# The Mamba front of a two-layer model on one core: five PSUM banks in a ring, one activation table set, and work for the scan moved ahead of the barrier

## What is computed

```python
xn = _layernorm(x, norm_w, norm_b)
xz = xn @ W_in                                   # 256 -> 2 x 512
x_ssm, z = jnp.split(xz, 2, axis=-1)
xc = conv(x_ssm, conv_w) + conv_b                # 4 taps per channel, causal
x_conv = silu(xc)                                # "u"
dt_low, B_mat, C_mat = jnp.split(x_conv @ W_x, [64, 80], axis=-1)
delta = jax.nn.softplus(dt_low @ W_dt + b_dt)
y = selective_scan(x_conv, delta, A, B_mat, C_mat, D)   # the second part of the block
y = y * silu(z)
```

## Time and profile before

| | us |
|---|---|
| median of 3 runs | 3569.22 (3567.5 to 3570.5) |
| the profiled execution | 3561.59 |
| its span in the profile | 3559.8 |
| end of the front's last sum, from the span's start | 252.6 |

### The profile page before, as it was taken

How to read it: one execution, slowest core, us unless ns; L and a number is a source line. 1 busy time by engine, 2 the same in 40 slices (tenths; PEclk the granted TensorE clock), 3 DMA queues, 4 the chain that set the end, 5 groups by cost and what they waited for, 6 DMA issues and landing times. The chain is left out here.

```text
span 3559.8 us, 54793 instructions
## 1 busy us (share of the span) xinstructions
PE 3222.1 (91%) x17996; PEld 1622.3 (46%) x18162; DVE 2750.6 (77%) x4129; ACT 2234.5 (63%) x3972; POOL 965.3 (27%) x907
## 2 busy tenths in 40 slices
PE   7868888988899998998799999999999999997897
PEld 3327777777566666775322222222222222224665
DVE  6739999999466664456888888888888888854666
ACT  5669999999100002222278888888788888883343
POOL 7639999998000000003200000000000000001100
PEclk9979999999899999999889999999999999998999
DMA  4656443420311416422400000000000000001001
GB/s 136 197 176 149 119 109 96 105 62 13 113 57 35 104 32 155 118 60 75 124 8 14 21 14 22 15 21 15 22 15 21 15 21 14 26 4 33 29 24 48
DMA packets 219079, 216.75 MB, mean 61 GB/s; under 512 B 63986, under 2 KB 165490, under 8 KB 218036
## 3 DMA queue, kind: packets, MB, share of 16 engines
q1 hardware_dynamic: 218820, 213.41, 21.9%
HBM read 145.99 MB, written 67.37 MB: 60 GB/s over the span
## 5 line engine op out<-in xcount | busy, mean ns | idle before, releaser
L1975 DVE TENSOR_REDUCE attn_part_max<-attn_pM 128x1 f32<-128x1024 f32 x1024 | 1204.4, 1219 | 162.8 <-PE attn_pM L2029 159.3
L1955 ACT ACTIVATE attn_probs<-attn_pE 128x512 f32<-128x512 f32 x2048 | 1089.8, 597 | 205.7 <-PE attn_pE L2078 196.4
L2078 PE MATMUL attn_pE<-attn_q,attn_k_exp 128*128 128x512 bf16 x1882 | 590.5, 385 | 54.6 <-ACT attn_q L1927 24.7
L2049 PE MATMUL attn_pA<-attn_probs,attn_v 128*32 128x512 f32 x4096 | 560.7, 604 | 2.0 <-issue 1.0
L648 DVE TENSOR_TENSOR_SCAN scan_h<-scan_abar,scan_states,scan_dbu 128x512 f32<-128x512 f32 x384 | 458.3, 1252 | 0.0
L2078 PEld LDWEIGHTS attn_pE<-attn_q,attn_k_exp 128*128 128x128 bf16 x2048 | 139.1, 97 | 609.0 <-ACT attn_probs L1955 462.4
L662 PE MATMUL scan_hT<-scan_ident,scan_h 128*128 128x128 f32 x2048 | 322.5, 281 | 71.3 <-ACT scan_hcT L600 29.0
L1908 POOL TENSOR_TENSOR attn_peak_parts<-attn_peak,attn_zero 128x4 bf16<-128x4 f32 x128 | 26.4, 206 | 1278.2 <-DVE attn_peak L1979 1278.2
L600 ACT ACTIVATE scan_hcT<-scan_hT,scan_c_t 128x512 f32<-128x512 f32 x512 | 366.4, 716 | 1.1 <-PE scan_hT L662 1.1
L2028 PE MATMUL attn_pM<-attn_k_exp,attn_q 64*128 64x512 bf16 x1024 | 326.1, 392 | 23.3 <-DVE attn_part_max L1975 15.1
L1173 PE MATMUL moe_pP<-moe_w_qkv,moe_xT 128*128 128x384 f32 x1024 | 340.3, 490 | 0.9
(11 more groups left out here) (282 smaller groups left out, 3874.4 us busy)
## 6 DMA issues: line engine op xcount, KB each, us to landing
scan_b_even<-mid_BC SPq DMA_DIRECT2D x16, 1024.0 KB, 10.2
scan_b_odd<-mid_BC SPq DMA_DIRECT2D x16, 1024.0 KB, 9.6
causal_rwB<-mid_rwT SPq DMA_DIRECT2D x64, 256.0 KB, 4.5
attn_q<-mid_q_parts SPq DMA_DIRECT2D x224, 64.0 KB, 2.4
mid_gT<-front_gT SPq DMA_DIRECT2D x8, 1024.0 KB, 8.4
mid_uT<-front_uT SPq DMA_DIRECT2D x8, 1024.0 KB, 9.7
mid_dT<-scan_g_odd SPq DMA_DIRECT2D x8, 1024.0 KB, 4.3
moe_yT<-mid_yT SPq DMA_DIRECT2D x7, 1024.0 KB, 6.7
```

What stands on the lines that cost most here:

```text
L1955: nc.scalar.activation(probs[:, kt % 4, h, :], pE[:, bank(item), :], ACT.Exp, scale=SCALE).then_inc(exp_done, 1)
L1975: nc.vector.reduce_max(part_max[:, h, j, i:i + 1], pM[:, m % 2, :], AXIS_X).then_inc(max_read, 1)
L2049: last = nc.tensor.matmul(pA[32 * h:32 * h + 32, :], v[:, par, kt, :], probs[:, kt % 4, h, :], start=(kt == 0), stop=(kt == KT - 1))
L2078: nc.tensor.matmul(pE[:, bank(item), :], k_exp[:, par, kt * 128:(kt + 1) * 128], q[:, qc, h, :], start=True, stop=True).then_inc(e_psum, 1)
```

## The change

It has four parts.

- **Ring of five.** pXZ has five banks. The products x, z and dt are numbered in the order in which PE makes them (`at_x`, `at_z`, `at_dt`), and product n uses bank n mod 5. `bank_free(n)` waits for those who read product n - 5.
- **One table set** ("natural_log_exp_and_others") is loaded ahead of Exp and serves Ln as well. The Silu set is loaded at ACT's start. Abs, Exp and Ln work in place in sp_log.
- **The norm** is a scalar_tensor_tensor, with the scale as a third operand that is broadcast along the row, in place of a tensor_scalar.
- **The end of the front.** The last sum (chunk 7) is made by DVE in four tiles, each behind its own Ln; the last store waits for those. POOL makes du behind the sum of chunk 6 and then the scan's first three dbu. ACT makes the decay behind the last Ln. The scan leaves these out.

```diff
+def scan_dbu(nc, pool, p, n):
+
+    pool.wait_ge(p.du_ready, 1)
+    pool.wait_ge(p.b_in[0][n // BQ], 16)
+    b_row = p.b_even[:, n, :].unsqueeze(1).broadcast_to([128, NDI, CH])
+    nc.gpsimd.tensor_tensor(p.dbu[:, n, :, :], p.du_even[:], b_row, ALU.mult).then_inc(p.dbu_ready, 1)
...
+    RING = 5
+    ROUND = 3 * NDI
+
+    def at_x(c, m):
+        return c * ROUND - NDI + m if c else m
+
+    def at_z(c, m):
+        return c * ROUND + NDI + m
+
+    def at_dt(c, m):
+        return c * ROUND + ROUND + m
...
-        sp_abs, sp_exp, sp_log, sp_relu = (s.sb(n, [128, NDI, CH]) for n in ("sp_abs", "sp_exp", "sp_log", "sp_relu"))
+        sp_log, sp_relu = s.sb("sp_log", [128, NDI, CH]), s.sb("sp_relu", [128, NDI, CH])
...
-        pXZ = s.ps("pXZ", [128, NDI, CH])
+        pXZ = s.ps("pXZ", [128, RING, CH])
...
                 def store_d(c):
-                    sp.wait_ge(d_ready, c + 1)
+                    if c == NCH - 1:
+                        sp.wait_ge(last_ready, NDI)
+                    else:
+                        sp.wait_ge(d_ready, c + 1)
...
-                    if c == NCH - 1:
-                        pool.wait_ge(following.unit_in[0], 32)
-                        nc.gpsimd.tensor_tensor(following.du_even[:], following.delta_even[:], following.u_even[:], ALU.mult).then_inc(following.du_ready, 1)
-                delta(NCH - 1)
+                pool.wait_ge(following.unit_in[0], 32)
+                nc.gpsimd.tensor_tensor(following.du_even[:], following.delta_even[:], following.u_even[:], ALU.mult).then_inc(following.du_ready, 1)
+                for n in range(NDBU):
+                    scan_dbu(nc, pool, following, n)
...
-                        ins = nc.vector.tensor_scalar(xn[:, c % 2, j, :], x[:, c % 2, j, :], mean[:, c % 2, j:j + 1], both[:, c % 2, j:j + 1], ALU.subtract, ALU.mult)
+                        ins = nc.vector.scalar_tensor_tensor(xn[:, c % 2, j, :], x[:, c % 2, j, :], mean[:, c % 2, j:j + 1], both[:, c % 2, j:j + 1].broadcast_to([128, D]), ALU.subtract, ALU.mult)
...
+                dve.wait_ge(d_out, (NCH - 1) * 16)
+                for m in range(NDI):
+                    dve.wait_ge(log_ready, (NCH - 1) * NDI + m + 1)
+                    dve.wait_ge(dt_relu, (NCH - 1) * NDI + m + 1)
+                    nc.vector.tensor_tensor(dT[:, m, :], sp_relu[:, m, :], sp_log[:, m, :], ALU.add).then_inc(last_ready, 1)
...
                     act.wait_ge(dt_read, (c + 1) * NDI)
+                    nc.scalar.preload_act_table_set("natural_log_exp_and_others")
                     for m in range(NDI):
-                        nc.scalar.activation(sp_exp[:, m, :], sp_abs[:, m, :], ACT.Exp, scale=-1.0).then_inc(exp_ready, 1)
-                    at_least(act, d_ready, c)
+                        nc.scalar.activation(sp_log[:, m, :], sp_log[:, m, :], ACT.Exp, scale=-1.0).then_inc(exp_ready, 1)
...
+                nc.scalar.preload_act_table(ACT.Silu)
                 act.wait_ge(in_loaded, 16 * 4)
...
+                    at_least(act, d_ready, c)
                     for m in range(NDI):
                         act.wait_ge(dt_relu, c * NDI + m + 1)
-                        nc.scalar.activation(sp_abs[:, m, :], pXZ[:, m, :], ACT.Abs, bias=b_dt[:, m:m + 1]).then_inc(dt_read, 1)
+                        nc.scalar.activation(sp_log[:, m, :], pXZ[:, at_dt(c, m) % RING, :], ACT.Abs, bias=b_dt[:, m:m + 1]).then_inc(dt_read, 1)
                 softplus(NCH - 1)
+                act.wait_ge(following.const_in, 32)
+                nc.scalar.activation(following.decay[:], following.a_log[:, :, 0:NS], ACT.Exp).then_inc(following.decay_ready, 1)
...
+                def bank_free(n):
+
+                    p = n - RING
+                    if p < 0:
+                        return
+                    c, r = divmod(p - NDI, ROUND)
+                    if c == NCH - 1 and NDI <= r < 2 * NDI:
+                        bank_free(p)
+                    elif p < NDI:
+                        pe.wait_ge(x_moved, p + 1)
+                    elif r < NDI:
+                        pe.wait_ge(g_ready, c * NDI + r + 1)
+                    elif r < 2 * NDI:
+                        pe.wait_ge(x_moved, c * NDI + r + 1)
+                    else:
+                        pe.wait_ge(dt_read, c * NDI + r - 2 * NDI + 1)
+                        pe.wait_ge(dt_relu, c * NDI + r - 2 * NDI + 1)
...
                     for m in range(NDI):
-                        at_least(pe, g_ready, (c - 1) * NDI + m + 1)
+                        bank_free(at_x(c, m))
```

More of the change, by code:

```diff
@@ L104 @@
 BQ = NS // 4
+NDBU = 3
 NE, HD = 16, 64
@@ L118, in scan_ahead @@
     s.delta_even, s.u_even, s.du_even = (s.sb(n, [128, NDI, CH]) for n in ("delta_even", "u_even", "du_even"))
-    s.const_in, s.du_ready, s.d_out = s.sem("const_in"), s.sem("du_ready"), s.sem("d_out")
+    s.dbu = s.sb("dbu", [128, NDBU, NDI, CH])
+    s.decay = s.sb("decay", [128, NDI, NS])
+    s.const_in, s.decay_ready, s.du_ready, s.dbu_ready, s.d_out = (s.sem(n) for n in ("const_in", "decay_ready", "du_ready", "dbu_ready", "d_out"))
     s.unit_in = [s.sem(f"unit_in_{par}") for par in ("even", "odd")]
@@ L371, in move_x @@
                             act.wait_ge(tail_ready, c)
-                    nc.scalar.activation(xs[:, c % 2, m, KC - 1:], pXZ[:, m, :], ACT.Identity).then_inc(x_moved, 1)
+                    nc.scalar.activation(xs[:, c % 2, m, KC - 1:], pXZ[:, at_x(c, m) % RING, :], ACT.Identity).then_inc(x_moved, 1)
                 def silu_z(c, m):
@@ L377, in silu_z @@
                         at_least(act, g_out, c * 16)
-                    nc.scalar.activation(gT[:, m, :], pXZ[:, m, :], ACT.Silu).then_inc(g_ready, 1)
+                    nc.scalar.activation(gT[:, m, :], pXZ[:, at_z(c, m) % RING, :], ACT.Silu).then_inc(g_ready, 1)
                 def silu_u(c, m):
@@ L446, in project_z @@
                     for m in range(NDI):
-                        if c == 0:
-                            pe.wait_ge(x_moved, m + 1)
-                        else:
-                            pe.wait_ge(dt_read, (c - 1) * NDI + m + 1)
+                        bank_free(at_z(c, m))
                         for k in range(KD):
-                            ins = nc.tensor.matmul(pXZ[:, m, :], w_in[:, k, DI + m * 128:DI + (m + 1) * 128], xnT[:, c % 2, k, :], start=(k == 0), stop=(k == KD - 1))
+                            ins = nc.tensor.matmul(pXZ[:, at_z(c, m) % RING, :], w_in[:, k, DI + m * 128:DI + (m + 1) * 128], xnT[:, c % 2, k, :], start=(k == 0), stop=(k == KD - 1))
                         ins.then_inc(z_psum, 1)
@@ L472, in _ @@
                     for m in range(NDI):
-                        if c + 1 < NCH:
-                            pe.wait_ge(x_moved, (c + 1) * NDI + m + 1)
-                        else:
-                            pe.wait_ge(g_ready, c * NDI + m + 1)
-                        nc.tensor.matmul(pXZ[:, m, :], w_dt[:, m * 128:(m + 1) * 128], xdbl[0:DTR, :], start=True, stop=True).then_inc(dt_psum, 1)
+                        bank_free(at_dt(c, m))
+                        nc.tensor.matmul(pXZ[:, at_dt(c, m) % RING, :], w_dt[:, m * 128:(m + 1) * 128], xdbl[0:DTR, :], start=True, stop=True).then_inc(dt_psum, 1)
         s.clear()
@@ L506, in selective_scan @@
     I_UNIT = NS * TPC
-    NDBU, NH, NHC = 3, 3, 8
+    NH, NHC = 3, 8
     LAST = UNITS * G_UNIT
@@ L512, in selective_scan @@
     with Scope(nc, "scan") as s:
-        ident, a_log = p.ident, p.a_log
-        decay, diag = s.sb("decay", [128, NDI, NS]), s.sb("diag", [128, NDI, 128])
+        ident, a_log, decay, dbu = p.ident, p.a_log, p.decay, p.dbu
+        diag = s.sb("diag", [128, NDI, 128])
         c_t = s.sb("c_t", [128, NT, NS])
@@ L519, in selective_scan @@
         g = [s.sb("g_even", [128, NDI, CH]), p.g_odd]
-        dbu = s.sb("dbu", [128, NDBU, NDI, CH])
         h = s.sb("h", [128, NH, NDI, CH])
@@ L583, in _ @@
                     for n in range(NS):
+                        if u == 0 and n < NDBU:
+                            continue
                         pool.wait_ge(du_ready, u + 1)
@@ L600, in evacuate @@
                     nc.scalar.activation(hcT[:, i % NHC, :], hT[:, i % 2, :], ACT.Copy, scale=c_t[:, u * TPC + tile, n:n + 1]).then_inc(hc_ready, 1)
-                act.wait_ge(const_in, 32)
-                nc.scalar.activation(decay[:], a_log[:, :, 0:NS], ACT.Exp).then_inc(decay_exp, 1)
-                act.wait_ge(decay_exp, 1)
-                nc.scalar.activation(decay[:], decay[:], ACT.Copy, scale=-1.0).then_inc(decay_ready, 1)
-                act.wait_ge(decay_ready, 1)
+                act.wait_ge(decay_ready, 2)
                 for k in range(LAST * NDI):
```

20 lines of the change are left out of this document (11 added, 9 removed).

## The result

The changed kernel took 3549.96 us, the median of five runs (3548.36 to 3554.12), against 3569.22 for the kernel before (3566.06 to 3570.5): ratio 0.9949, 95% interval 0.9938 to 0.996. That is 19.3 faster; 17 was predicted.

The account below looks back on a forecast made before the run. A loop over ACT and PE was taken to bound the kernel, with stores taking gain back. End 15.1, behind the barrier 1 and start 0.7 sum to 17: 3569.2 - 17 = 3552, range 3540 to 3565.

Parts of the forecast that it names:

- The loop: Over ACT and PE: round 27.2 to 22.5, PE's hole ahead of x 3.50 to about 0.5; three rounds gain 13.9.
- The stores: ACT's Silu of chunks 4, 5 and 6 waits for SP's store of gT, 2 to 4 each; gain there 14.5.
- t(0): Turn of chunk 0, the start of ACT's Exp table load: 51.92 in the kernel before; t(c) likewise for chunk c.
- Rival B: Stores never hold ACT: six rounds of 22.5, gain 31 + 1.7, time 3536; chance 0.12.
- The norm and the sum: Three-operand norm lengthens DVE's chain by 1.6; POOL's sum waits behind both, ending 15.3 after the turn instead of 13.7.
- rival D: Slower: POOL's xr and sum each stop DVE, rounds 26.9, or 31.6 if the norm loses one too; 3591; chance 0.06.
- The end: Ahead of the barrier POOL is last, after du and three dbu, 185.6 after t(0); gain 15.1.
- exclusion: At the front's end DVE's tiles and POOL's dbu exclude each other; 4 x 0.7 added to POOL's end.
- Behind the barrier: The DMA for c_t may find dT's last store out of its way: 0 to 2, taken as 1.
- The start: Preload saves 1.28, less 0.6 for the first norm held by POOL's xr: net 0.7, bounds -3.6 and +1.3.
- rival C: The ring buys nothing: rounds of 25.9, gain 6, time 3563; chance 0.24.
- slow clock: PE's x at the lower clock level behind a long hole: priced at 1.6, none charged behind a hole of 0.5.

Follow-up runs that it names:

- the repeat: The changed kernel run once more with no edit, beside the experiments: 3545.98 us, ratio 0.9944 to the kernel before.
- the reordered versions: Changed kernel with SP storing gT ahead of dT and b loads: 3537.83; with dbu in the scan 3533.73, also without ring 3540.02; with ring, uT early too 3528.60.
- three-dbu experiment: Changed kernel with the first three dbu made in the scan again, du staying in the front: 3546.35 us, ratio 0.9934.
- the version with gT first: Changed kernel with SP storing gT ahead of dT and the loads for the scan: 3537.83 us, ratio 0.9915.

## Why the prediction was right

**The loop.** Rounds of 22.5 were forecast, 22.42 came, with a hole of 0.29 for 0.5. The three free rounds gained 81.47 - 67.25 = 14.2 (13.9 forecast).

**The stores.** Counted from t(0) = 50.48, Silu of chunks 4, 5 and 6 came at 77.4, 106.4 and 134.3 (forecast 78.3, 106.2, 134.0), t(6) at 151.2 (151.1). A fit this close is partly luck: in the repeat t(6) came at 147.9, and its waits of 5.88 and 1.52 lie outside the forecast 2 to 4. That the stores take it back because of their place in SP's order, and not because the DMA engines are full, is shown by moving two of them: the waits went from gT to uT, and then vanished, with the same bytes. Rival B (stores never hold, 3536) is what the reordered versions are; this kernel is not.

**The norm and the sum.** The size was nearly right (the sum ends 14.6, 14.5 and 15.3 after the turns of chunks 2 to 4, for 15.3), but the reason in the first two was another. There xr stood beside the convolution (8.79 instead of 4.91) until the chain was over, and the sum followed at once, so the norm waited for the sum. The forecast order, the sum behind chain and norm, is the row at 151.75, where it took 9.60. The prediction's rival D had xr and sum each stopping DVE. What happened is mostly DVE stopping xr, which cost nothing, and one stop of the norm a round, in rounds that stayed 22.42, so it did not delay ACT or PE. The Trainium skill ("SBUF — State Buffer", Who interferes with whom) says that a VectorE instruction with two SBUF inputs contends with a GpSimd instruction that reads SBUF. The trace agrees: the convolution has two SBUF inputs, and both xr and the sum took longer beside it. That the norm is held in either form is what the rows say.

**The end.** POOL was forecast last, 185.6 after t(0), from an exclusion of 4 x 0.7. The end came at 235.56 - 50.48 = 185.1, but it was DVE's. Of the first two tiles each waited for a dbu (they took 2.79 and 4.98 instead of some 0.7), and POOL waited hardly at all (13.88 for three dbu, 4.63 each, for 4.5). The tiles ended 13.0 after the turn instead of the 6.4 that the prediction gives them. The number was right by offsetting errors: the exclusion was priced on the wrong engine and too low there, and the last turn came 1.2 earlier than forecast (172.1 for 173.3), with PE's dbl in that round at 5.34 instead of 6.61 behind a hole of 4.07 instead of 5.49. The three-dbu experiment shows the exclusion's full size: 5.5 to 6.4 of tile duration (8.1 in the version with gT first).

**Behind the barrier** 1 was forecast from an earlier DMA of the C rows, with dT's store out of its way. This gain was absent: the third step stands 248.15 - 237.47 = 10.68 behind the issue of that DMA, as 10.69 before, and dT's store, issued when DVE's last tile is done, is still ahead of it. Moving the dbu ahead gained nothing there, as forecast: in all the versions, with them or without, the distance is 10.55 to 10.71.

**The start** gained 1.44 instead of 0.7, just outside the bound of 1.3: xr did not hold the first norm (1.81). In the repeat t(0) was 51.27, a gain of 0.65.

**The signs.** Nine table loads fewer came (16 for 25 in the front, none at the scan's start), and so did the split x and the waits for gT in the first profile. Two signs went against the forecast: POOL was not last, and two tiles stood for a POOL instruction in the last round, one of them for nearly the whole of it (4.98), which comes close to what the prediction had listed as a sign of being wrong. They touch its account of the end, not that of the loop.

**The step that was mis-sized** is the assumption under rival C, that without the ring rounds would be 25.9. They are 24.2 mostly. The 1.6 of slow clock was tied to the ring in the sum, but the hole of 2.1 that the tables alone leave saves it in most rounds. The sum was right because the changed kernel has both; the worth of each part was not. Within the 19, tables and ring are not additive: 0.9954 and 0.9955 alone, 0.9949 together.

## What to carry to other kernels

When a loop gets shorter, work out for each transfer that it waits for when that one would land, from its place in the queue; here that gave the time of the changed kernel within 3 us, and it also named the next edit, which with the dbu put back brought as much again (18 to 20). Try the halves of a change apart: two of them can each be worth all of it. An instruction moved ahead of a barrier "because its engine is free" can hold up the engine that is not: here four tiles of 2.50 took 8 to 10.6.

## What was not expected of the hardware

**The clock and the length of a hole.** This counts x from x(2) on, each of which has a z ahead of its hole (the very first x is slow in every profile, behind 1.60 or 2.88, with little work on PE before it). Behind every hole of PE of 3.5 or more, x was slow: 8.5 to 9.8 for sixteen matmuls instead of 7.1 (behind the hole of the earlier trace rows with the granted clock at 0.59, so mostly at the lower level of 1.2 GHz), 6.96 to 8.47 for twelve instead of 5.42. Behind 2.53, in the repeat, it was slow too (7.11 for twelve). Behind 2.08 and 2.09 it was slow three times (8.80 for sixteen) and thirteen times not (7.10 or 7.11), in three different kernels, once in each. Behind 1.85 and less it never was. What decides in the middle case stays open.

**How POOL and DVE share SBUF.** POOL's xr, with one tensor from SBUF, is held beside DVE's two-input chain as the sum is (8.79 for 4.91). A chain of short DVE instructions holds POOL off over many of them (the sum at 151.75 took 9.60, until chain and norm were over), while POOL's products of 4.6 to 4.7 each let one DVE instruction in between (norms, tiles). Why the sum at 151.75 didn't get in between two instructions of the chain stays open.

**The last stage's clock and length differ between executions of one kernel.** The windows of the last 345 us (busy time of PE, PEld, DVE, ACT, POOL, then the granted clock), first the kernel before in its first profile, then in its second:

```profile
3214.80:3559.80 345.00, 289.32 (x1299) 203.18 (x1297) 220.45 (x540) 127.78 (x176) 28.57 (x16) 0.93 0.10 34
```

```profile
3222.50:3567.50 345.00, 293.16 (x1286) 205.38 (x1285) 219.33 (x538) 126.69 (x174) 26.73 (x15) 0.90 0.11 34
```

At 0.93 granted, the lookup (from POOL's first instruction in it to the end) took 346.0 in the one, at 0.90 it took 352.8 in the other; the changed kernel has 0.91 and 349.6. All thirteen profiles fall in this order: 346.0 at 0.93, 347.1 at 0.92, 349.6 to 349.9 at 0.91 (four), 352.8 to 353.8 at 0.90 (seven); the kernel before stands near both ends. This is 3.6 of the 5.5 by which the first two spans differ less than the third steps; the rest lies in the stages between. So single spans cannot be compared more closely than this. The clock and the length go together; what sets that clock was not tried.
